# Left-over rows of a mixture-of-experts stage: from gathered mixed tiles to lists per expert copied in DRAM

## The reference

```python
x = x + attention(layernorm(x), ctx, ctx)          # causal, per sequence
xt = layernorm(x).reshape(8192, 128)
logits = xt @ gate_w.T                              # 8 experts
_, idx = top_k(logits + beta, 2)
probs = sigmoid(take_along_axis(logits, idx))       # the weights of the two experts of a token
h = silu(xt @ gate_proj[e]) * (xt @ up_proj[e])     # 128 -> 256
eo[e] = h @ down_proj[e]                            # 256 -> 128
x = x + sum over the two chosen e of probs * eo[e] + shared_expert(xt)
```

## Time and profile before

| | us |
|---|---|
| median of 3 runs | 432.77 (430.17 to 433.64) |
| span of the profiled execution, first to last instruction | 435.0 |
| TensorE busy in it | 393.7 |
| VectorE / ScalarE / GpSimd busy | 292.4 / 240.3 / 255.6 |
| adds to the output on GpSimd, 64 | 100.4 |
| scatters, 64 / gathers, 27 | 64.6 / 26.1 |

### The profile page before, as it was taken

The page is one execution under the profiler, slowest core; times in us unless marked ns, Lnnn a source line. Parts: engine busy times, 40 slices in busy tenths (PEclk is TensorE's granted clock), DMA queues, the critical chain, the costliest instruction groups (busy, mean ns, idle before and its releaser), DMA issues.

```text
span 435.0 us, 11130 instructions
## 1 busy us (share of the span) xinstructions
PE 393.7 (91%) x3325; PEld 327.7 (75%) x3325; DVE 292.4 (67%) x1273; ACT 240.3 (55%) x570; POOL 255.6 (59%) x317
## 2 busy tenths in 40 slices
PE   8888999999799798796877789999999999999994
PEld 3444666657455564686867689999999999999993
DVE  5877998897697486564654366666667766666663
ACT  3696989879687462334343356666311256666550
POOL 7758788785688577046878855555420005555554
PEclk9999999999999899898989989999999999999999
DMA  7973337793221112225557763333333212332222
GB/s 218 357 226 120 123 130 232 229 265 125 67 92 52 64 50 82 87 69 120 97 86 88 72 95 45 48 52 51 49 58 71 52 27 36 49 49 32 26 26 24
DMA packets 43049, 41.78 MB, mean 96 GB/s; under 512 B 5688, under 2 KB 31808, under 8 KB 42992
## 3 DMA queue, kind: packets, MB, share of 16 engines
q1 hardware_dynamic: 30864, 30.69, 24.4%
q0 software_dynamic: 12128, 10.40, 17.5%
HBM read 24.17 MB, written 16.90 MB: 94 GB/s over the span
## 4 chain that ended last, share of the span: by engine, by line
PE 53%; POOL 5%; DVE 5%; issue 4%; another core or an unknown queue 2%; POOLq 1%; ACT 0%; DVEq 0%; ACTq 0%
PE gu_pair L1710 32%; PE bank L1734 16%; POOL sorted_rows L495 3%; PE bank L1676 2%; DVE t_hid L1275 1%; PE bank L1649 1%; POOL rstd L455 1%; PE bank L1637 1%; POOL out L546 1%; PE bank L1628 0%; DVE hid L1106 0%; ACT rows L734 0%; POOLq L493 0%; DVE x L1025 0%
## 5 line engine op out<-in xcount | busy, mean ns | idle before, releaser
L546 POOL DMA_INDIRECT out<-t_out,tile_in x64 | 100.4, 1569 | 108.0 <-DVE t_out L1315 100.2
L1710 PE MATMUL gu_pair<-tile_T,W_slot 128*128 128x128 f32 x1024 | 129.5, 280 | 1.5 <-issue 0.9
L1710 PEld LDWEIGHTS gu_pair<-tile_T,W_slot 128*128 128x128 f32 x1024 | 123.6, 197 | 1.9 <-issue 1.7
L831 ACT ACTIVATE t_silu<-gu_pair 128x512 f32<-128x512 f32 (+1 forms) x78 | 46.4, 594 | 125.7 <-PE gu_pair L1710 109.5
L1734 PE MATMUL bank<-W_down,t_hid 128*128 (+1 forms) x620 | 84.6, 280 | 14.1 <-DVE t_hid L1275 14.1
L1275 DVE SCALAR_TENSOR_TENSOR t_hid<-t_silu,gu_pair 128x512 f32<-128x512 f32 (+1 forms) x78 | 53.2, 683 | 62.6 <-PE gu_pair L1710 29.9
L1734 PEld LDWEIGHTS bank<-W_down,t_hid 128*128 128x128 f32 x620 | 76.7, 195 | 16.2 <-issue 16.2
L495 POOL DMA_INDIRECT sorted_rows<-rows,slot x64 | 64.6, 1009 | 21.8 <-issue 20.7
L821 ACT ACTIVATE W_slot<-W 128x512 f32 x128 | 73.0, 621 | 3.4 <-DVE slot_pair L1166 2.0
L506 POOL DMA_INDIRECT left_in<-sorted_rows,left_index x27 | 26.1, 967 | 23.0 <-DVE left_index L1193 15.0
L1649 PE MATMUL bank<-shared_dn,hid 128*128 128x128 f32 x256 | 34.6, 293 | 1.0 <-DVE hid L1106 0.9
(11 more groups left out here) (160 smaller groups left out, 551.2 us busy)
## 6 DMA issues: line engine op xcount, KB each, us to landing
tile_in<-sorted_rows SPq DMA_DIRECT2D x91, 66.5 KB, 1.9
x_sb<-x SPq DMA_DIRECT2D x16, 256.0 KB, 5.0
c_T<-ctx_cols SPq DMA_DIRECT2D x16, 256.0 KB
c_sb<-ctx SPq DMA_DIRECT2D x16, 256.0 KB
out<-acc SPq DMA_DIRECT2D x16, 256.0 KB
sorted_rows<-padding SPq DMA_DIRECT2D x1, 2128.0 KB, 13.0
sorted_rows<-left_in SPq DMA_DIRECT2D x27, 66.5 KB
sorted_rows<-rows,slot POOLq DMA_INDIRECT x64
```

What stands on the lines that cost most here:

```text
L546: e.indirect_dma_start(out_flat, bass.IndirectOffsetOnAxis(ap=tile_in[:, tiles_of(i)[0] % NR, ID:ID + 1].bitcast(I32), axis=0), t_out[:, q ...
L831: e.activation(t_silu[:, 0:n * M], gate_up_pair[i % 2][0][:, 0:n * M], ACT.Silu).then_inc(s_t_silu, 1)
L1710: r = e.matmul(bank[:, c:c + P], w, tile_T[:, i % TX, tile], start=True, stop=True, skip_group_check=True)
```

## The change

The left-over rows are no longer gathered. Each of the 28 pair lists' last part is copied from DRAM to DRAM twice by SP: into a list of its lower expert (kind 1) and into one of its higher expert (kind 2). There are 7 + 7 such lists. Each copy moves 128 rows, the valid ones and what lies behind; the next copy to the same list starts where the valid rows end and waits until the one before has landed, and a pad of 128 zero rows closes the list. The tiles of all lists of a kind, at most 33 (ENTRIES), are run with one expert each, two tiles in a unit (17 units, DUALS), and both experts' outputs of a token are added to the output by separate DMAs. The two weights stand in the row in the order lower, higher expert (ROW = 131), so no comparison is needed. Padding rows carry token numbers of the first 13 tiles and weight 0. The order of units (WORK = 71): 14 full tiles (HEAD), 17 units of kind 1 with 11 full tiles among them, the same for kind 2, 1 full tile (TAIL). There are 37 + 66 = 103 tiles and as many adds. NR becomes 20, NO 14; the two drains come after adds 13 and 58. The tables of left-overs and extras go, those of lists come. pair_path() becomes pairs_of().

```diff
-    ROW = D + 1 + 2 * K
+    ROW = D + 1 + K
+    HEAD = 14
+    TAIL = 1
+    order = [(0, p) for p in range(HEAD)]
+    for k in (1, 2):
+        among = (FULL - HEAD - TAIL) // 2
+        for d in range(DUALS):
+            order.append((k, d))
+            if (d + 1) * among // DUALS > d * among // DUALS:
+                order.append((0, sum(kind == 0 for kind, _ in order)))
...
-        NR, AHEAD, TX, TW, NO, NL = 16, 6, 3, 8, 12, 6
+        NR, TX, NO = 20, 3, 14
...
             def load_tile(n):
...
+                    e.wait_ge(s_t_added[n % NR], added(n - NR))
+                if order[slot_with[n]][0] and tiles[slot_with[n]][0] == n and order[slot_with[n]][1] == 0:
+                    k = order[slot_with[n]][0] - 1
+                    for l in range(LISTS):
+                        e.wait_ge(s_listed[l], listed(k, l, parts_of(k, l) + 1))
+                    e.wait_ge(s_none_out, 16 * (1 + NONES))
...
+            def copy_part(k, c):
...
+                if k or r:
+                    e.wait_ge(s_listed[l], listed(k, l, r))
+                e.dma_start(sorted_rows[bass.DynSlice(part_at[k, r, l], P, STRIDE), :],
+                            sorted_rows[bass.DynSlice(P + part_of(k, r, l), P, STRIDE), :]).then_inc(s_listed[l], 16)
+
+            def pad_list(k, l):
...
+                e.wait_ge(s_listed[l], listed(k, l, parts_of(k, l)))
+                e.dma_start(sorted_rows[bass.DynSlice(pad_at[k, l], P, STRIDE), :], padding[:, l]).then_inc(s_listed[l], 16)
...
-                for j in range(done, upto):
-                    store_left(j)
+                if n == HEAD - 1:
+                    fill_lists(0, len(parts[0]) + LISTS)
+                    for j in range(NONES):
+                        e.dma_start(sorted_rows[bass.DynSlice(NONE + j * STEP, P, STRIDE), :],
+                                    padding[:, LISTS + j]).then_inc(s_none_out, 16)
+                if n >= HEAD:
+                    fill_lists(1, 1)
...
-            def gather_left(j):
...
+                if order[i] == (1, 0) and n == tiles[i][0]:
+                    for m in range(PADS):
+                        e.wait_ge(s_t_added[m], added(m))
+                if order[i] == (2, 0) and n == tiles[i][0]:
+                    last = max(m for m in range(n) if order[slot_with[m]][0] == 1)
+                    for m in range(last - NR + 1, last + 1):
+                        e.wait_ge(s_t_added[m % NR], added(m))
...
-            for q in range(SLOTS):
-                for j in range(gathered, left_before(q)):
-                    gather_left(j)
-                gathered = left_before(q)
-                add_to_out(q)
+            for n in range(TILES):
+                add_to_out(n)
+                if n in DRAINED:
+                    e.drain()
...
-                e.tensor_scalar(index, top_index[:, :, 0:K], CODE, None, ALU.add).then_inc(s_index, 1)
+                for k, op in enumerate((ALU.min, ALU.max)):
+                    r = e.tensor_tensor(index[:, :, k], top_index[:, :, 0], top_index[:, :, 1], op)
+                r.then_inc(s_index, 1)
...
             def tile_out(i):
...
+                if kind:
+                    for h, n in enumerate(tiles[i]):
+                        free_out(n)
+                        e.tensor_scalar(t_out[:, n % NO], y[:, h * D:(h + 1) * D], tile_in[:, n % NR, WT + kind - 1:WT + kind], None,
+                                        ALU.mult).then_inc(s_t_out, 1)
                     return
...
+            list_consts()
             tile_table()
...
-            left_table()
-            tile_weights(0)
-            for i in range(PAIRS + 1):
+            list_ranges()
+            list_tables_of_entries()
+            for i in range(WORK + 1):
...
-                if i + 1 < PAIRS:
-                    tile_weights(i + 1)
```

More of the change, by code:

```diff
@@ L16, with pairs_of @@
 MASKED = -1e30
[L19 to L25, removed]
+def pairs_of(E):
+    return [(a, b) for a in range(E) for b in range(a + 1, E)]
 def build(nc, x, ctx_in, ctx_cols, gate_w, beta, gate_proj, up_proj, down_proj, shared_gate, shared_up,
@@ L65, in build @@
     assert T == 64 and D == P and M == 2 * P and E == 8
[L67 to L70, removed]
+    HEAD = 14
+    TAIL = 1
+    assert PADS < HEAD
+    order = [(0, p) for p in range(HEAD)]
[5 more added lines that the diff above has]
+                order.append((0, sum(kind == 0 for kind, _ in order)))
+    for _ in range(TAIL):
+        order.append((0, sum(kind == 0 for kind, _ in order)))
+    assert sum(kind == 0 for kind, _ in order) == FULL
+    WORK = len(order)
     x_rows = x.rearrange("b s d -> (b s) d").rearrange("(g p t) d -> g p t d", g=G, t=GT)
@@ L160, in build @@
         ends = sb("ends", [P, Q])
[L161 to L169, removed]
+        sizes = sb("sizes", [P, Q])
+        until = sb("until", [P, Q])
@@ L254, in left_before, with entries @@
-        def left_before(q):
-            return min(4 + 2 * q, LT)
-        def outs_until(i):
-            return tiles_of(i)[-1] + 1
-        s_const, s_pairs, s_fresh, s_warm = sem("const"), sem("pairs"), sem("fresh"), sem("warm")
+        list_tables = tile_pair[0][:, 2 * P:2 * P + 4 * TABLED].rearrange("p (n j) -> p n j", n=4)
+        def entries(i):
+            kind, d = order[i]
+            return [] if kind == 0 else list(range(2 * d, min(2 * d + 2, ENTRIES)))
+        tiles = []
+        for i in range(WORK):
+            first = tiles[-1][-1] + 1 if tiles else 0
+            tiles.append(list(range(first, first + max(len(entries(i)), 1))))
@@ new lines, in build, with halves, parts_of, listed @@
+        TILES = tiles[-1][-1] + 1
+        slot_with = {n: i for i in range(WORK) for n in tiles[i]}
+        def halves(i):
+            return [0, 0] if order[i][0] == 0 else list(range(len(tiles[i])))
+        def parts_of(k, l):
+            return LISTS - l if k == 0 else l + 1
+        def listed(k, l, r):
+            return 16 * (r if k == 0 else parts_of(0, l) + 1 + r)
+        def part_of(k, r, l):
+            return path.index((l, l + 1 + r) if k == 0 else (r, l + 1))
+        parts = [[(r, l) for r in range(LISTS) for l in range(LISTS) if r < parts_of(k, l)] for k in range(2)]
@@ L360, in load_rows @@
[L360 to L369 removed]
+                kind = order[slot_with[n]][0]
@@ L963, in scalar_program @@
             copy_first_tile_T(1)
-            for i in range(PAIRS):
+            for i in range(WORK):
                 silu(i)
-                if i + 2 < PAIRS and slot_of(i + 2) is not None:
-                    copy_W(slot_of(i + 2))
+                if i + 2 < WORK:
+                    copy_W(i + 2)
         def vector_program(e):
@@ L1724, in tile_down @@
                 else:
-                    e.wait_ge(s_t_out, outs_until(i - 2))
-                for h, (_, extra) in enumerate(passes(i)):
+                    e.wait_ge(s_t_out, tiles[i - 2][-1] + 1)
+                for h in range(len(halves(i))):
                     y = Y_pair[i % 2][:, h * D:(h + 1) * D]
```

628 lines of the change are left out of this document (275 added, 353 removed).

## The result

The changed kernel took 427.39 us (median of 4 runs, 426.45 to 429.54) where the kernel before took 432.50: a ratio of 0.989, 95% interval 0.985 to 0.993. So it is faster by 1.1%, or 5 us, where 13.8 were forecast. The profiled execution took 426.79 us with a span of 425.1, which puts 1.7 us around a span.

What follows compares the result with a forecast made beforehand. TensorE was taken to bind the kernel after a slow head, and POOL's adds the changed one: add 14 at 247.3 + 165.5 + 2.8 + 2.8 − 0.3 + 3.1 = 421.2 of span, 419.0 us on the median; range 402 to 440.

Steps and rivals of the forecast that it cites:

- the likeliest case: From unit 14 on, 89 adds queue on POOL at 1.86 us each and set the end: 409 to 428 us; chance 0.50.
- the −2.2 us that turned the span into a time: The earlier profile's span, 435.0, was 2.2 us above the median 432.77, so span 421.2 became time 419.0.
- the drain after add 13: POOL's drain before the first list tile's add: said to lie in the wait for that tile, at no cost.
- the end behind the last add: From the queue's end on POOL to the program's end: 3.1 us.
- Unit 0: Start of the tile stage: 186.94 + 2.0 = 188.9 us, for added DVE work in choose() and list_consts().
- The head and the lists: SP's copies, pads and empties before tile 14's load take 35 us; unit 14 starts at 240, not 232.9.
- the head's loss: Units 0 to 17 lose 22.9 us: 4.9 before unit 5 is kept, 18.0 goes with the gathers.
- The queue: POOL from add 14 at 247.3: 165.5 us of adds, 2.8 for a wait, 2.8 for a drain, less 0.3.
- Rival A: POOL doesn't bind and PE sets the end: span 407.5 down to 400.4, time 398 to 405; chance 0.12.
- Rival B: The slow head stays, as gathers aren't its cause; unit 14 at about 243 + 2, span 426, time 424; chance 0.15.
- C: Lists come too late, as SP's copies land slowly before tile 14's load: at 7 us a landing, 451; chance 0.13.
- D: DMA engines slow the first list phase: 28 units at 4.1 us take 115 instead of 82, time 452; chance 0.10.

Runs made afterwards that it cites:

- b_again: The kernel before, unchanged, run once more for a second profile on the slower kind of chip: 432.89 us with a span of 431.1.

## Why the prediction was right in kind and wrong in size

The tile stage alone, from unit 0's gate matmuls to the end of the span:

| | kind S | kind F |
|---|---|---|
| kernel before | 248.1 (first trace), 245.7 (b_again) | 224.9 |
| changed kernel | 239.9 | 239.7 |
| with 32 adds less | not run | 224.2 |
| forecast, changed | 232.3 | |

The changed kernel's stage takes the same time on either kind; what differs is the kernel before. The range held the time, and the likeliest case, adds that queue on POOL, is the one that happened. The gain was forecast as 13.8 us and is 5.1. The steps that failed are terms of the sum: the −2.2 us that turned the span into a time (it is +1.7), the drain after add 13, put at nothing (2.0), and the end behind the last add, 3.1 (6.0). In all the size was off by 8.4 us (427.4 against 419.0), and it splits so:

- **From span to time, +3.9.** "2.2 us above the median" took one high profiled execution for a property of the span. A time is its span plus 1.7 or 1.8 in each run here; −2.2 stood where +1.7 belonged. By 421.2 + 1.7 the forecast would have been 422.9, 9.9 us under the median before. A further 0.6 lies between the median and the profiled run.
- **Unit 0, −3.7.** Forecast 188.9, measured 185.21. The list operations on DVE and the ordering in choose(), 2.0 together, cost nothing that can be seen beside b_again's 185.40 (on kind F 0.5 to 0.9: 173.06 and 173.49 against 172.58), and the first trace had its unit 0 1.5 us late.
- **The head and the lists, +3.0 from unit 0 to unit 14.** This takes back most of the −3.7: unit 14 hangs on the lists and not on unit 0, and it started at 239.31 where 240 was forecast. All of the head's loss went, also the 4.9 us before unit 5 that the forecast kept (units 0 to 12 take 33.5 us, 12 × 2.79), which made no odds, as the lists came later. That unit 14 is so close is partly luck, since errors cancel on its path: SP was free for the copies at 190.50 instead of 193, issued for 36.6 us (to 227.06) instead of 35, PE's transposes followed after 6.0 instead of 7, unit 14 after another 6.2 instead of 5; pads and empties came out as said (7.1). Within the 36.6 the forecast was wrong: it had the later rounds bound by landing. In the trace of SP's waits only 1.1 and 1.4 us of it are waits for a copy to land (0.8 for padding comes behind it); the rest is issuing, 0.71 us a copy (0.52, and 0.19 to the next) and register loads. So nearly all of the 28 copies are bound by the issuing queue. The last copy was issued at 217.37 and the pad that waits for it at 219.87, so it landed within 2.5 us; a store to an empty tile took 1.8. The Trainium skill's page "DMA: Bandwidth & Descriptors" ("Anatomy of one DMA — SWDGE (gpsimd) path") has about 2 us fixed for a DMA issued by GpSimd, most of it the write receipt, which is heaviest where the target is HBM. These two, issued by SP and ending in DRAM, are near it.
- **The drain after add 13, +2.0.** "Lies in the wait for the first list tile" was wrong: add 13 itself comes late, at 243.32, since tile 13 is held up with tile 14 (PE transposes two units ahead). So the drain stands behind it and the first list add comes 9.3 us behind its gate, not 7.3. The add's row puts its gap down to t_out, but DVE had written that at 245.20; the drain's own record (the first of two) runs 4.2 us from 243.1, and the waits for 13 landed adds follow it:

```profile
245.20 0.61 DVE L1272 TENSOR_SCALAR t_out<-bank,tile_in 128x128 f32<-128x128 f32 x2
L739 POOLq DRAIN  x2: 4217/4856/5496, 243.1 to 331.5; - x2
```

- **The queue, −0.3.** 88 steps of 1.86, one add and 5.5 us of stops: 170.5 us, forecast 170.8. Within it the wait took 1.4 instead of 2.8 and the drain 4.1 instead of 2.8.
- **The tail, +2.9.** 425.1 − 419.11 = 6.0 us from the last add's end to the end of the span, forecast 3.1 by the earlier trace rows. With 32 adds less, most of them spaced, it was 397.1 − 392.44 = 4.7. That fits adds that take longer to land when they stand back to back; their landings aren't in the traces.

Rival A fell: without 32 of the adds, and so without the queue, the time is 16.1 us less on kind F. Its own number was too low as well, because PE alone needs 224.2 us from unit 0, where the forecast had 407.5 − 188.9 = 218.6. Rival B's number, 426 of span, came within 1 us of the 425.1 measured, by chance: its slow head didn't happen. It was half right in something else: on these runs a slow head takes both the gathers and kind S. C did not happen, as no landing was long. D fell on the row of 262 to 311 us: PE full at a DMA share of 0.71.

What the prediction could not see from one trace is that the 18 us of the head's loss that it gave to the gathers are there on one kind of chip only. On kind F the account is: without the queue of adds the stage takes 224.2 us against 224.9, so the hole before the lists, the slow matmuls behind it and a longer tail eat all but 0.7 of what fewer passes save (18.8 by the forecast's count); the queue then adds 239.7 − 224.2 = 15.5.

## What to carry to other kernels

Before a queue of small DMAs is added, multiply its count by the issuing engine's time per DMA and set that against the stage. Here 103 adds × 1.86 = 192 us for POOL against 199 us of TensorE work left no room for the stretches in which POOL had to idle. Move the point at which a prefetch begins apart from the point at which its result is used: HEAD 18 with the copies moved along gave 2.2 us (kind S), HEAD 18 with the copies left in place 5.7 (kind F), HEAD 20 so 8.4 (kind F) and 7.9 (kind S). And a gain that rests on stalls with no named cause is to be measured on more than one chip, and counted from a common event within the program.

## What the runs showed of the hardware

- **Two kinds of chip, 8% apart for one program, with VectorE, ScalarE and GpSimd equally busy.** 397.5 against 431.1 us of span; 12.8 in stage 1 and 20.8 in the tile stage. Every trace of S has waits with "remote" for their end, 21 to 34 us before unit 0, and no trace of F has one. In the tile stage of S these waits and PE's stalls come with the gathers and go with them, while the DMA share hardly differs (0.64 and 0.67). Which part of the chip it is stays open, and whether it lasts: no run here separates the DMA queues, the memory or the fetching of instructions, and none tried the scatters of stage 1.
- **An indirect add costs POOL nearly all by the DMA, not by the row:** 1.55 us for 128 rows, 1.42 for 64.
- **A drain of POOL behind queued adds costs 4.1 us** (337.70 − 331.71 − 1.86) where the trace of before had 2.8 behind spaced ones.
- **A copy within DRAM of 128 rows costs SP 0.71 us of issue,** 28 of them 27.4 us with their register loads and one short wait.
